# A two-layer convolution and matching-pursuit kernel: shorter statistics, the dictionary prepared beside image 0, gathers without a wait for landings

## The reference, cut to what matters

```python
x = x + conv3x3_circular(_gn(x), weight)        # 16 x 64 x 128 x 128, 64 -> 64
x = x + _L1_conv_ref(_gn(x), dictionary)        # dictionary 1024 x 512

def _L1_conv_ref(z, dictionary):
    D = dictionary / (norm(dictionary, axis=0) + EPS)
    X = patches_4x4(z).T                         # 1024 x (B * 32 * 32)
    coeffs = batch_omp(X, D)                     # 5 atoms a patch
    return unpatch((D @ coeffs).T)

def batch_omp(X, D):
    G = D.T @ D + DIAG_EPS * eye(N);  h_bar = (D.T @ X).T
    for k in range(1, 6):
        index = argmax(abs(h * ~mask), axis=1)   # next atom of each patch
        # a row more of the Cholesky factor from G[I, index], triangular solves
        h = h_bar - einsum('bk,bkn->bn', x_stack, G[I])
```

## Time and profile before

| | |
|---|---|
| median of 2 runs | 3583.23 us (3581.29 to 3585.17) |
| profiled execution | 3581.48 us, its span 3579.5 us |
| PE busy | 3067.3 us (86%) |
| DVE busy | 2579.2 us (72%) |
| ACT busy | 2367.6 us (66%) |
| POOL busy | 1856.7 us (52%) |
| DMA | 428.38 MB, mean 120 GB/s |

### The profile page before, as it was taken

One profiled execution on the slowest core, in us unless ns is written; L12 is line 12 of the kernel. 1 busy time (PEld: TensorE's weight loads), 2 busy tenths in 40 slices (PEclk: granted clock), 3 DMA queues, 4 the chain that ended last, 5 costly groups with the idle time before them and its releaser, 6 DMA issues.

```text
span 3579.5 us, 35041 instructions
## 1 busy us (share of the span) xinstructions
PE 3067.3 (86%) x9488; PEld 1310.8 (37%) x9488; DVE 2579.2 (72%) x6596; ACT 2367.6 (66%) x3795; POOL 1856.7 (52%) x1861
## 2 busy tenths in 40 slices
PE   6796889899898989989898989989898998986617
PEld 2232333343333334333333434333333433332303
DVE  2027887878788687878778786878778777887872
ACT  3535686858677676858668685767768576765634
POOL 0015565555555564655656555555655555556651
PEclk8998999999999989999999999999999999997858
DMA  3433443534354343434444353445435344442222
GB/s 114 154 108 117 136 132 97 180 84 145 102 163 132 124 139 91 156 91 154 133 141 131 101 177 73 151 114 158 127 109 163 86 144 102 127 106 60 59 59 47
DMA packets 131028, 428.38 MB, mean 120 GB/s; under 512 B 55696, under 2 KB 55952, under 8 KB 106128
## 3 DMA queue, kind: packets, MB, share of 16 engines
q0 software_dynamic: 91136, 202.10, 23.3%
q1 hardware_dynamic: 39696, 224.05, 17.1%
HBM read 289.70 MB, written 136.31 MB: 119 GB/s over the span
## 4 chain that ended last, share of the span: by engine, by line
PE 49%; DVE 15%; issue 10%; ACT 10%; POOL 8%; DMA 5%; ACTq 0%; POOLq 0%; SPq 0%; DVEq 0%
PE gen_ps L909 22%; PE gen_ps L918 15%; PE conv_ps L952 8%; POOL v L479 7%; DVE u L832 6%; ACT hot L543 4%; PE conv_ps L959 4%; DMA u<-marked_rows,chosen 4%; DVE idx L732 2%; DVE h L840 2%; DVE top L723 2%; ACT score L617 1%; ACT junk_sums L356 1%; ACT ct L530 1%; ACT z L567 1%
## 5 line engine op out<-in xcount | busy, mean ns | idle before, releaser
L479 POOL DMA_INDIRECT v<-gram_rows,cell x1280 | 1278.2, 999 | 919.3 <-DVE cell L741 392.4
L909 PE MATMUL gen_ps<-ct,dt 128*128 128x512 f32 x2048 | 948.1, 618 | 69.6 <-ACT rb L555 60.3
L918 PE MATMUL gen_ps<-dn,z 128*128 128x512 f32 x2048 | 927.9, 607 | 62.4 <-ACT z L567 50.8
L952 PE MATMUL conv_ps<-xh,wc 128*128 128x512 f32 x1536 | 717.1, 617 | 91.0 <-ACT xa L585 83.5
L491 POOL DMA_INDIRECT u<-marked_rows,chosen x504 | 506.1, 1004 | 492.8 <-DVE chosen L737 329.0
L723 DVE MAX8 top<-score 128x8 f32<-128x512 f32 x640 | 420.7, 691 | 294.6 <-ACT score L617 278.5
L909 PEld LDWEIGHTS gen_ps<-ct,dt 128*128 128x128 f32 x2048 | 400.5, 198 | 583.2 <-issue 571.2
L918 PEld LDWEIGHTS gen_ps<-dn,z 128*128 128x128 f32 x2048 | 389.9, 194 | 568.0 <-issue 512.9
L832 DVE SCALAR_TENSOR_TENSOR u<-u,nl 128x512 f32<-128x512 f32 x748 | 514.2, 747 | 95.4 <-DMA u<-marked_rows,chosen 92.6
L617 ACT ACTIVATE score<-h 128x512 f32<-128x512 f32 x640 | 377.6, 604 | 241.3 <-DVE h L840 120.4
L655 DVE SCALAR_TENSOR_TENSOR ce<-hot,xc,ce 128x512 f32<-128x512 f16 x512 | 365.1, 745 | 159.1 <-ACT hot L546 159.1
(11 more groups left out here) (103 smaller groups left out, 1870.5 us busy)
## 6 DMA issues: line engine op xcount, KB each, us to landing
xh<-x_paired SPq DMA_DIRECT2D x128, 650.0 KB, 4.0
xa<-x_pairs SPq DMA_DIRECT2D x64, 1024.0 KB, 6.1
y_rows<-xa SPq DMA_DIRECT2D x64, 1024.0 KB, 6.3
y_rows<-rb POOLq DMA_DIRECT2D x64, 1024.0 KB, 8.3
v<-gram_rows,cell POOLq DMA_INDIRECT x1280
u<-marked_rows,chosen POOLq DMA_INDIRECT x504, 3.8
dn<-atoms SPq DMA_DIRECT2D x1, 2048.0 KB, 7.8
gram_rows<-u SPq DMA_DIRECT2D x4, 256.0 KB, 2.0
```

Source lines behind the costliest of these rows:

```text
L479: pool.indirect_dma_start(v[:, g, k - 1, j, t:t + 1], None, cells, bass.IndirectOffsetOnAxis(ap=cell[:, g, k // (KMAX - 1), j, t:t + 1], a ...
L909: last = pe.matmul(to[:], dt_[:, a, d, :], ct[:, a, :], start=(a == 0), stop=(a == NA - 1))
L918: last = pe.matmul(to[:], z[:, t % 2, d // PATCH, d % PATCH, :], dn[:, d, :], start=(d == 0), stop=(d == ND - 1))
L952: pe.matmul(conv_ps[:, a], wc[:, tap, a * CIN:a * CIN + P], rows[:, a + 1:a + 2 * CP:2, tap:tap + W], start=(tap == 0), stop=False)
```

## The change

1. The statistics: a copy more on ACT lets one `average` matmul carry five columns; `spread` goes, the root takes three ACT steps, DVE's chain five steps instead of nine.
2. The dictionary: in `setup` the image is loaded first and the atoms last, and only the statistics of image 0 and `tap_sum` stay there. Norms, scaling and Gram blocks move into period 0 (after evacuations 0 and 2, after `convolve` 1, 4 and 5, before `average` and the first `correlate`), the transposes of the atoms into period 1, after each `convolve`. POOL writes the two tables, ahead of its periods.
3. `settle` goes: POOL issues a unit's gathers when its cells and atoms are there.
4. New plans for ACT, DVE and POOL, a new order of `recon`, `turn` and `convolve` on PE, banks to match. `bias` now stands before `correlate` 3.

```diff
 VECTOR_PLAN = {
-    1.5: [("co", 0)], 3: [("ce", 0, 0)], 10.5: [("ce", 0, 1)], 23.5: [("co", 1)], 24: [("ce", 1, 0)],
-    30: [("ce", 1, 1), ("gn", 1, 1)], 31: [("gn", 1, 2), ("gn", 1, 3)], 37: [("gn", 0, 1)],
-    39.5: [("gn", 0, 2), ("gn", 0, 3), ("gn", 0, 4)],
+    0.5: [("co", 0)], 3: [("ce", 0, 0)], 10: [("ce", 0, 1)], 24: [("co", 1), ("ce", 1, 0)],
+    30: [("ce", 1, 1), ("gn", 1, 1)], 37.5: [("gn", 0, 1)], 39.5: [("gn", 0, 2)],
 }
...
 SCALAR_PLAN = {
-    0: [("z", 4), ("oh", 0, 0, 1)],
-    3: [("ev", 0), ("oh", 0, 1, 1), ("oh", 0, 0, 2), ("oh", 0, 1, 2), ("oh", 0, 0, 3), ("oh", 0, 1, 3),
-        ("oh", 0, 0, 4), ("oh", 0, 1, 4), ("ev", 1), ("z", 5), ("ct", 0, 0)],
-    5: [("z", 6)], 7: [("ev", 2), ("oh", 0, 2, 1)], 8: [("oh", 0, 3, 1)],
-    11: [("oh", 0, 2, 2), ("oh", 0, 3, 2), ("oh", 0, 2, 3), ("oh", 0, 3, 3), ("oh", 0, 2, 4), ("oh", 0, 3, 4),
-        ("oh", 1, 0, 1), ("ct", 0, 1), ("ev", 3), ("st", 10), ("st", 11), ("st", 12), ("st", 0), ("ev", 4)],
-    13: [("oh", 1, 1, 1)],
-    15: [("oh", 1, 0, 2), ("ct", 0, 2), ("h", 4), ("oh", 1, 1, 2), ("st", 13), ("z", 7), ("h", 5), ("h", 6),
-        ("ct", 0, 3)],
-    17: [("st", 1)], 19: [("ev", 5), ("st", 2)], 21: [("h", 7)],
-    23: [("st", 3), ("st", 14), ("re", 0, 0), ("st", 4), ("re", 0, 1), ("st", 5), ("re", 0, 2), ("oh", 1, 0, 3),
-        ("oh", 1, 1, 3), ("ev", 6), ("oh", 1, 0, 4), ("oh", 1, 1, 4), ("st", 6), ("re", 0, 3), ("oh", 1, 2, 1),
-        ("oh", 1, 3, 1), ("oh", 1, 2, 2)],
-    25: [("oh", 1, 3, 2), ("st", 15)],
-    27: [("re", 0, 4), ("ev", 7), ("re", 0, 5), ("re", 0, 6), ("re", 0, 7), ("ct", 1, 0)],
-    31: [("st", 16), ("st", 17), ("oh", 1, 2, 3), ("oh", 1, 3, 3), ("oh", 1, 2, 4), ("ct", 1, 1), ("oh", 1, 3, 4),
-        ("ct", 1, 2), ("ct", 1, 3), ("rt", 1), ("re", 1, 0), ("z", 0), ("z", 1), ("st", 7), ("re", 1, 1),
-        ("re", 1, 2), ("st", 8)],
-    32: [("z", 2)], 35: [("h", 0), ("re", 1, 3), ("h", 1)], 36: [("z", 3), ("re", 1, 4), ("re", 1, 5)],
-    37: [("h", 2), ("re", 1, 6)], 39: [("rt", 0), ("h", 3), ("re", 1, 7)],
+    0: [("oh", 0, 0, 1), ("oh", 0, 1, 1)],
+    3: [("z", 4), ("oh", 0, 0, 2), ("ev", 0), ("oh", 0, 1, 2), ("oh", 0, 0, 3), ("oh", 0, 1, 3), ("oh", 0, 0, 4),
+        ("oh", 0, 1, 4), ("oh", 0, 2, 1), ("oh", 0, 3, 1), ("z", 5), ("ev", 1), ("ct", 0, 0)],
+    7: [("ev", 2)], 8: [("oh", 0, 2, 2)],
+    11: [("oh", 0, 3, 2), ("oh", 0, 2, 3), ("oh", 0, 3, 3), ("oh", 0, 2, 4), ("oh", 0, 3, 4), ("ct", 0, 1),
+        ("ev", 3), ("z", 6), ("oh", 1, 0, 1), ("st", 10), ("st", 11), ("z", 7), ("oh", 1, 1, 1), ("oh", 1, 0, 2)],
+    13: [("ev", 4), ("ct", 0, 2)], 15: [("st", 12), ("st", 13), ("oh", 1, 1, 2), ("h", 4), ("ct", 0, 3), ("st", 0)],
+    17: [("h", 5), ("h", 6), ("ev", 5)], 20: [("st", 1)], 21: [("st", 2), ("h", 7)],
+    23: [("st", 3), ("ev", 6), ("st", 4), ("re", 0, 0), ("re", 0, 1), ("st", 5), ("st", 14), ("oh", 1, 0, 3),
+        ("oh", 1, 1, 3), ("oh", 1, 0, 4), ("oh", 1, 1, 4), ("re", 0, 2), ("ev", 7), ("re", 0, 3), ("oh", 1, 2, 1),
+        ("oh", 1, 3, 1)],
+    24: [("st", 15)], 25: [("oh", 1, 2, 2)], 27: [("re", 0, 4), ("st", 16), ("st", 17), ("ct", 1, 0)],
+    30: [("rt", 1)],
+    31: [("oh", 1, 3, 2), ("ct", 1, 1), ("oh", 1, 2, 3), ("oh", 1, 3, 3), ("oh", 1, 2, 4), ("oh", 1, 3, 4),
+        ("re", 0, 5), ("ct", 1, 2), ("re", 0, 6), ("ct", 1, 3), ("z", 0), ("re", 0, 7), ("st", 6), ("st", 7),
+        ("st", 8), ("z", 1), ("re", 1, 0), ("re", 1, 1)],
+    35: [("h", 0), ("re", 1, 2), ("re", 1, 3), ("z", 2), ("z", 3), ("h", 1), ("re", 1, 4), ("re", 1, 5), ("rt", 0)],
+    36: [("re", 1, 6), ("re", 1, 7)], 39: [("h", 2), ("h", 3)],
 }
...
 ADD_PLAN = {
-    4: [(0, 0)], 5: [(0, 1)], 7: [(1, 0)], 9: [(1, 1)],
+    4: [(0, 0)], 6: [(0, 1)], 7: [(1, 0)], 9: [(1, 1)],
 }
...
 TAIL_VECTOR_PLAN = {
-    0: [(2, ("co", 0))], 10: [(2, ("ce", 0, 0))], 17.5: [(2, ("ce", 0, 1))], 21.5: [(2, ("co", 1))],
-    22.5: [(2, ("ce", 1, 0))], 27: [(2, ("ce", 1, 1))], 43.5: [(1, ("co", 0))], 44: [(1, ("ce", 0, 0))],
+    1.5: [(2, ("co", 0))], 10: [(2, ("ce", 0, 0))], 13.0: [(2, ("ce", 0, 1))], 24: [(2, ("co", 1))],
+    27: [(2, ("ce", 1, 0))], 33.0: [(2, ("ce", 1, 1))], 43.5: [(1, ("co", 0)), (1, ("ce", 0, 0))],
...
+
+                act.activation(mv[:, n, 2:5], avg[:, P:], ACT.Copy, scale=mv[:, n, 0:1]).then_inc(gn_ready[n], 1)
...
-            def settle(img, g, k):
-
-                if k < KMAX - 1:
-                    pool.wait_ge(row_loaded[g][T - 1], at(img, 16 * (KMAX - 1), 16 * (k + 1)))
-                else:
-                    pool.wait_ge(v_last[g], at(img, 16 * T * k, 16 * T * k))
...
                     if here[back]:
-                        if gathered:
-                            settle(*gathered[-1])
-                        gathered.append((i - back, g, k))
                         gather(i - back, g, k)
...
+                    if i == 0 and c == 0:
+                        act.wait_ge(atoms_in, 16)
+                        for d in range(ND):
+                            act.activation(u[:, d // 2, d % 2, :], dn[:, d, :], ACT.Square).then_inc(squared, 1)
+                    elif i == 0 and c == 2:
+                        act.wait_ge(summed, 1)
+                        act.activation(norm[0], gen_ps[2][:], ACT.Sqrt).then_inc(rooted, 1)
...
+                        act.wait_ge(turned, c + 1)
+                        act.activation(dt_[:, a, half * 4:half * 4 + 4, :], ct_ps[:], ACT.Copy).then_inc(turned_copied, 1)
...
             def root(image, n):
-                act.wait_ge(gn_step[n], at(image, GN_STEPS, 5))
-                act.activation(gsc[n][:, 4:5], gsc[n][:, 3:4], ACT.Sqrt).then_inc(gn_root[n], 1)
+                gs = gsc[n]
+                act.wait_ge(gn_sum[n], at(image, GN_SUMS[n], 1))
+                act.activation(gs[:, 6:9], st_ps[:, 5 * n + 2:5 * n + 5], ACT.Square, accum_out=gs[:, 0:1]).then_inc(gn_root[n], 1)
+                act.wait_ge(gn_root[n], at(image, GN_ROOT, 1))
+                act.activation(gs[:, 1:2], st_ps[:, 5 * n + 1:5 * n + 2], ACT.Identity, bias=gs[:, 0:1]).then_inc(gn_root[n], 1)
+                act.wait_ge(gn_root[n], at(image, GN_ROOT, 2))
+                act.activation(gs[:, 2:3], gs[:, 1:2], ACT.Sqrt, bias=eps[:, 0:1]).then_inc(gn_root[n], 1)
...
                 if part == 1:
-                    dve.wait_ge(gn_sum[n], at(i, GN_SUMS[n], 1))
...
+                    dve.wait_ge(gn_root[n], at(i, GN_ROOT, GN_ROOT))
+                    dve.reciprocal(gs[:, 3:4], gs[:, 2:3]).then_inc(gn_step[n], 1)
...
-                elif part == 2:
-                    dve.wait_ge(gn_sum[n], at(i, GN_SUMS[n], 2))
-                    dve.tensor_scalar(gs[:, 3:4], st_ps[:, 3 * n + 1:3 * n + 2], GN_EPS, None, ALU.add).then_inc(gn_step[n], 1)
...
+                    dve.reciprocal(fac[par][:, n, 0:1], gs[:, 5:6]).then_inc(gn_step[n], 1)
...
-            for part in (1, 2, 3, 4):
+            for part in (1, 2):
                 gn_part(0, 0, 0, part)
+            normalise_atoms()
+            for a in range(NA - 1):
+                gram_rows(a)
...
             def correlate(i, back, t):
+                if i == 0 and t == 0:
+                    gram_block(NA - 1)
+                    pe.wait_ge(gram_copied, 4 * NA - 3)
...
+            def norms():
+
...
+                    last = pe.matmul(gen_ps[2][:], ones, u[:, d // 2, d % 2, :], start=(d == 0), stop=(d == ND - 1))
...
+            def gram_block(a):
+                if a == 0:
+                    pe.wait_ge(scaled, ND)
...
+            def turn_atoms(n):
...
+                    last = pe.transpose(ct_ps[:, m, :], dn[:, half * 4 + m, a * P:(a + 1) * P], ident[:])
...
-            def spread(i, n):
...
+                if i == 0 and n == 1:
+                    gram_block(2)
+                pe.wait_ge(gn_ready[n], at(i, 2, 2))
+                pe.matmul(st_ps[:, 5 * n:5 * n + 5], avg[:, 0:P], mv[:, n, :], start=True, stop=True).then_inc(gn_sum[n], 1)
...
                 last.then_inc(conv_done, 1)
+
+                if i == 0 and c == 1:
+                    norms()
+                elif i == 0 and c in (4, 5):
+                    gram_block(c - 4)
+                elif i == 1:
+                    turn_atoms(c)
...
                     correlate(i, 1, 7)
                 if p:
                     recon(i, 2, 0, 0)
+                if own:
+                    convolve(i, 6)
+                if p:
                     recon(i, 2, 0, 1)
                 if own:
-                    convolve(i, 6)
+                    convolve(i, 7)
                 if p:
                     recon(i, 2, 0, 2)
                     recon(i, 2, 0, 3)
                     recon(i, 2, 0, 4)
-                if own:
-                    convolve(i, 7)
-                if p:
+                    turn(i - 2, 1, 0)
                     recon(i, 2, 0, 5)
                     recon(i, 2, 0, 6)
                     recon(i, 2, 0, 7)
-                    turn(i - 2, 1, 0)
-                    turn(i - 2, 1, 1)
```

(29 more changed lines are left out.)

220 lines of the change are left out of this document (104 added, 116 removed), and 68 rows, old and new, of tables (BANKS, TAIL_SCALAR_PLAN).

## The result

| | before | after |
|---|---|---|
| median | 3583.23 us | 3542.65 us (3542.37 to 3542.93, 2 runs) |
| profiled execution, its span | 3581.48, 3579.5 us | 3542.37, 3540.5 us |

The ratio is 0.9881, interval 0.9861 to 0.9901: 40.6 us faster, 1.1%. The forecast was 3505, its range 3455 to 3568; the time lies in the range, but the gain is under the 2% that the forecast called "faster" and gave the larger chance. About half of the forecast gain came.

What follows compares the result with a forecast made beforehand. No engine bounds it everywhere: in a full period PE is busy 186 of 205 us, with a chain through other engines between its stretches. 3581.5 - 20 (start) - 48 (14 periods) - 9 (tail) gives 3505; range 3455 to 3568.

Steps and rivals of the forecast that it cites:

- Set-up: Before image 0: image loaded first, dictionary last, so conv 0 starts at 42 us, 38.7 earlier; moved work paid inside image 0.
- Period 1: Second image's period: transposes mostly hide behind evacuations, evacuation 7 comes 3 us later; +5 us, leaving the start at -20.
- Steps 1 to 4 of the new orders: Full period, reordered ACT and PE: first u gather at 50.8, evacuation 3 49.0, correlate 7 76.3, third pair's `ce` 110.3.
- the slow rival: Full period: evacuation 4 behind scores that wait for gathered rows, late landings delay conv 5; 3651 us, chance 0.08.
- step 2: Full period: evacuation 3 at 49.0 instead of 52.0, no 2.82 us idle before conv 4, rows land at 57.9.
- Step 5: Full period's end: last pair's `ce` ends at 140.6 instead of 144.5, recon (1,0) starts at 143.4 instead of 146.4.
- the forecast's own signs: Full period: prediction wrong if PE waits for evacuation 4 before conv 5, or if periods stay at 205 us.
- Step 6: Full period from recon (1,0) to next conv 0: same PE work, 58.5 us less 0.4 for the bias matmul; period 201.5.
- The rival that counts the gathers in full: All periods: the 5.65 us gather wait is on the path, -6.5 us a period; 3458 us, chance 0.20.
- The sign for it: Dropping the gather wait: POOL without waits for DMA, DVE's waits for u rows almost the same; 0 to 1 us a period.
- Tail: After the full periods: an 8 us `ce` leaves the chain and gather waits go; -9 us, bounds -4 and -14.
- period unchanged: Full period closes at the same length, rows landing at 60.4, evacuation 6 waiting for conv 6; 3552 us, chance 0.26.

Runs made afterwards that it cites:

- e1_ct_late: The changed kernel with `ct` (1,0) and the root `rt` (1) moved behind the scores of unit 7 in ACT's plan: 3496.64 us, ratio 0.9767.

## Why the prediction was right or wrong

**Set-up: right.** Statistics of image 0 were said to be ready at 35.5 and were at 35.46; conv 0 of image 0 was put at 42 and came at 41.37; of image 1 at 180, came at 179.34. The Gram blocks, norms and squares were paid inside image 0 as summed.

**Period 1: cause and size wrong.** +5 for the transposes, which cost next to nothing: PE reaches the statistics of image 1 at 110.3 from conv 0, before it was 113.0. But the period grew by 9.6, of which the rows after show:

```profile
300.71 9.79 PE L975 MATMUL gen_ps<-dn,z 128*128 128x512 f32 x16 [10.50 <-ACT z L577]
310.33 0.28 PE L1012 MATMUL conv_ps<-mv,avg 128*128 128x5 f32 x2
325.87 16.01 PE L975 MATMUL gen_ps<-dn,z 128*128 128x512 f32 x32 [15.26 <-ACT h L588]
```

Correlate 1 now shares its bank with correlate 0 and waits 15.26 for that one's copy out; before, it had another bank and didn't wait, and only correlate 2 did, 3.67. Correlate 0 waits 10.50 for z0, before 6.06. In full periods recons fill this time; period 1 has none. I had read the new banks for the full period only.

**Steps 1 to 4 of the new orders: right, to within 0.7 us.** `ce` of the first pair ends at 18.2 (said 18.4), first u gather 50.4 (50.8), evacuation 3 done at 48.8 (49.0), no idle before convolve 4 and 5.33 for its first 12 matmuls, correlate 7 at 77.0 (76.3; it waits for h4, not z7), convolve 6 done at 95.5 (94.8), `ce` of the third pair at 110.5 (110.3). Evacuation 4, the place of the slow rival, costs PE 0.96 us. The landing in step 2 came with a twist: unit 3 was to wait for its rows until 57.9, and did start on them at 58.6, but the wait that ends last is the one for v entries, at 56.6. These were in time before (0.28 us of wait).

**Step 5 failed: "PE is through recon 7 at 127 already".** It was at 132.0, and `ce` of the last pair ended at 144.9 instead of 140.6, later than before (144.5). The step counted PE's matmuls and left out what recon 7 has to wait for: the bank of recon 4, that copy's buffer `rb`, and the write out of it, which starts only when recon 3 has been copied. This copy moved by 1.5 us only (from 115.6 to 114.1), as recon 3 now stands behind convolve 7, and the write behind it took 1.4 us longer to land. The 4.3 us by which `ce` misses its mark arise between there and `ce`. Where e1_ct_late takes the scores out of this line, `ce` ends at 141.8 and the period is 201.7, near the forecast's own 201.5: what the forecast had of the rest of the period was right, to about 1 us.

By the forecast's own signs it was wrong here: periods stayed at 205. PE does stand before conv 5 for evacuation 4, the other sign, but for 0.96 us only.

**The sum: a size off, and a wide range.** The 48 us of the period were counted from one period of 204.94, but the 14 take 205.8 on average; at 201.5 each they would have given 60. e1_ct_late shows it: it hits the period and comes to 3496.6, 8 us under the forecast's 3505. That the changed kernel's 3542.7 lies inside 3455 to 3568 is due to the width of that range, which reached over the unchanged period of 3552, and not to the forecast's own mechanism for the period.

**Step 6: right.** From recon (1,0) to the next conv 0 it said 58.1 and it is 57.5.

**`settle`: not tested by itself where the kernel before takes 3580, blind beside that.** The rival that counts the gathers in full (-6.5 a period, 3458) falls: typical periods didn't move. e1_ct_late comes to 201.7 as the orders alone were to give it, which fits 0 to 1 us a period for the gathers, but no run there separates the two. The sign for it came half true: POOL waits for no landing, but DVE's waits for u rows didn't stay almost the same; they fell from 98 to 12 us, and those for v entries grew. By itself the missing wait was measured only where the kernel before takes 3890, and there it loses 3%. No row of the profile before tells of that. The forecast's slower rival had said that rows could land later without spacing, but what it would cost was put down to evacuation 4, which is another mechanism.

**Tail: right in sum** (-10.0 for -9), not shown in its parts.

Of the rivals, "period unchanged" (0.26, 3552) came nearest in number, and its period is the one that was measured, for a like reason, DVE setting PE's stall in the middle; but the cause it named (rows at 60.4, evacuation 6 late) was not the one.

## What to carry to other kernels

When a reordering brings one engine forward, look for the transfer that doesn't move with it: follow each item that the forecast puts earlier back to its buffers (who has to read it empty, when was that read issued, how long does it take to land), not only to the engine before it. A wait for a landing is cheap if what stands behind it in that engine's order can wait, so try first to move the urgent items ahead of it: here moving two items in one engine's order gave 1.1% more (ratio 0.9767 after 0.9881), as much again as the whole change. Ask too which other transfers the reordering brings next to it: here two writes came ahead of it, and it took longer. When a gain is multiplied by a number of periods, take the average period and not one. And when a wait is taken away that only spaces transfers, time it on more than one chip.
